# Attention scores in strips of 64 columns: another tiling of the products, another grouping of the heads, and the band's edge cleared by GpSimd for four units

## What is computed

```
dist = q_pos[:, :, None] - k_gpos[:, None, :]
allowed = (dist > 0) & (dist <= w) & (k_gpos[:, None, :] >= 0)
scores = jnp.einsum('bhnqd,bhnkd->bhnqk', qb, kb) * scale
scores = jnp.where(allowed, scores, NEG)
attn = jax.nn.softmax(scores, axis=-1)
out = jnp.einsum('bhnqk,bhnkd->bhnqd', attn, vb)
```

## Time and profile before

| | |
|---|---|
| median of 3 runs | 621.35 us (620.0 to 621.54) |
| the profiled execution: its time / its span | 620.31 us / 618.6 us |
| busy in the span: PE, DVE, POOL, ACT | 571.3, 448.0, 344.9, 290.6 us |
| mean granted TensorE clock | 0.965 of full |

### The profile page before, as it was taken

One profiled execution on the slowest core, in us unless ns is written; L12 is line 12 of the kernel. 1 busy time (PEld: TensorE's weight loads), 2 busy tenths in 40 slices (PEclk: granted clock), 3 DMA queues, 4 the chain that ended last, 5 costly groups with the idle time before them and its releaser, 6 DMA issues. The chain is left out here.

```text
span 618.6 us, 17277 instructions
## 1 busy us (share of the span) xinstructions
PE 571.3 (92%) x5504; PEld 390.2 (63%) x5509; DVE 448.0 (72%) x2031; ACT 290.6 (47%) x787; POOL 344.9 (56%) x749
## 2 busy tenths in 40 slices
PE   7898869979999999899999999987799999999992
PEld 3555336747777677577777777754367766776672
DVE  6884458838888888688888888885464767766646
ACT  1464305727676676567776767773132121212110
POOL 4664202637885878658888588898212242432251
PEclk9997979969999999899999999998999999999997
DMA  4586850633542454255433440000000000000001
GB/s 132 176 259 180 200 111 9 133 50 46 59 52 41 50 66 50 30 54 63 49 45 52 59 58 11 4 2 1 2 2 0 2 19 17 17 0 17 19 18 34
DMA packets 56590, 33.83 MB, mean 55 GB/s; under 512 B 5850, under 2 KB 55426, under 8 KB 56506
## 3 DMA queue, kind: packets, MB, share of 16 engines
q1 hardware_dynamic: 55450, 32.45, 29.0%
q10 hardware_dynamic: 1056, 0.35, 0.2%
HBM read 21.18 MB, written 11.27 MB: 52 GB/s over the span
## 5 line engine op out<-in xcount | busy, mean ns | idle before, releaser
L1036 DVE CUSTOM_DVE_ANT_0 added<-psS,maskq 128x256 bf16<-128x256 f32 x512 | 205.5, 412 | 61.1 <-PE psS L893 53.7
L1267 ACT ACTIVATE probs<-psST 128x512 f32<-128x512 f32 x256 | 154.0, 603 | 109.5 <-PE psST L914 108.3
L914 PE MATMUL psST<-qst,kst 98*128 98x128 bf16 x1024 | 101.7, 222 | 5.0 <-DMA qst<-mT 4.7
L914 PEld LDWEIGHTS psST<-qst,kst 98*128 98x128 bf16 x1024 | 79.1, 99 | 28.0 <-DMA qst<-mT 6.7
L893 PE MATMUL psS<-kst,qst 68*128 68x256 bf16 x448 | 88.6, 280 | 1.3 <-DVE rowmax L1036 0.8
L930 PE MATMUL psPV<-probs,vst 128*9 128x128 f32 x2048 | 82.2, 280 | 0.8 <-POOL probs L1182 0.4
L1179 POOL TENSOR_SCALAR_AFFINE_SELECT probs<-probs 128x256 f32<-128x256 f32 x140 | 57.9, 413 | 33.9 <-ACT probs L1267 33.7
L1700 ACT ACTIVATE hT<-fpsH 128x512 f32<-128x512 f32 x32 | 19.1, 598 | 121.6 <-PE fpsH L1444 121.6
L1182 POOL TENSOR_SCALAR_AFFINE_SELECT probs<-probs 128x256 f32<-128x256 f32 x140 | 57.4, 410 | 0.0
L893 PEld LDWEIGHTS psS<-kst,qst 68*128 68x128 bf16 x448 | 35.0, 102 | 33.7 <-issue 22.3
L1441 PE MATMUL fpsH<-xehi,w1hi 128*128 128x512 f32 x128 | 55.7, 435 | 0.0
(11 more groups left out here) (179 smaller groups left out, 1144.3 us busy)
## 6 DMA issues: line engine op xcount, KB each, us to landing
qst<-q_parts SPq DMA_DIRECT2D x96, 64.0 KB
kst<-k_parts SPq DMA_DIRECT2D x96, 64.0 KB
q_parts<-split SPq DMA_DIRECT2D x8, 384.0 KB, 2.7
k_parts<-split SPq DMA_DIRECT2D x8, 384.0 KB, 2.9
v_tok<-vt SPq DMA_DIRECT2D x8, 288.0 KB, 3.3
vst<-v_tok SPq DMA_DIRECT2D x16, 144.0 KB
X<-in_L_attn_x_dram SPq DMA_DIRECT2D x8, 256.0 KB, 3.0
out_dram<-res SPq DMA_DIRECT2D x8, 256.0 KB, 2.2
```

Source lines behind the costliest of these rows:

```text
L914: last = nc.tensor.matmul(bank[:, a, side * P:(side + 1) * P], kst[0:KALL, h, ring(n - 1 + side)], qst[0:KALL, h, ring(n)], start=not mask ...
L1036: taken = nc.vector.tensor_tensor_reduce(added[:, h], psS[g % 2][:, a], mask[:], 1.0, NEG * 4, ALU.add, ALU.max, rowmax[:, n.mod(2), h:h + 1])
L1267: nc.scalar.activation(probs[:, g], psST[g % 2][:].rearrange("p a c -> p (a c)"), ACT.Exp, scale=SCALE).then_inc(s_exp.sem, 1)
```

## The change

`scores` computes each head in two strips of 64 queries by 192 keys, the only keys that the band of such a strip can touch, instead of one 128 by 256. `scores_t` computes strips of 64 keys by 64 or 128 queries; the corners of a bank that no strip covers hold NEG, written once by DVE. The mask product covers the two 64-column edges only, and SELECTED has four units (0, 2, 4, 6). Units now pair other heads (`head_of`), so that `values` takes two heads at once: v of 18 columns by 256 probabilities, two calls of four units each (at g = 5 and at g = 1 of the next step) where there were four calls. The maximum reads 192 columns. Only the first block of each sequence is special, not every eighth. q, k and v are written to DRAM in another order and are loaded for four blocks at once in rows of 8 KB; for that the columns of the weights are rearranged by ten ACT copies, v's bias comes with eight DMAs, and `project` is no loop any more. The DMAs for the masks are small. Many waits and places move; those that the prediction speaks of are in the diff, cut to its core:

```diff
-LC = 2
+LC = 4
+SLOTS = RING // LC
+HALF = H // 2
 STORES = 16 * 4
-LOADS = 14
-PARTS_Q = [0, 0, 0, 1, 1, 2]
-PARTS_K = [0, 1, 2, 0, 1, 0]
+RUNS_Q = ((0, 0, 3), (3, 0, 2), (5, 0, 1))
+RUNS_K = ((0, 0, 1), (1, 0, 1), (2, 0, 2), (4, 1, 2))
+LOADS = 16 * (len(RUNS_Q) + len(RUNS_K))
...
+QD = 64
+QUADS = P // QD
+WIN = P + QD
 UN = H // 2
-SELECTED = (0, 2, 3, 4, 6)
+SELECTED = (0, 2, 4, 6)
 EPS = 1e-5
 LN_EPS = 1e-12
+
+
+def head_of(g, a):
+
+    return H // 2 * (g // 4) + 4 * a + g % 4
...
+def load_half(sp, c, half, side, held, scratch, s_half):
+
+    u, heads = c % SLOTS, slice(half * HALF, (half + 1) * HALF)
+    tile, runs = ((held.qst, RUNS_Q), (held.kst, RUNS_K))[side]
+    rows = scratch[side][c].rearrange("a (d h) t -> (a d) h t", h=H)[:, heads].rearrange("r h t -> r (h t)")
+    for first, part, parts in runs:
+        sp.dma_start(tile[first * HD:(first + parts) * HD, u, heads].rearrange("r h t -> r (h t)"),
+                     rows[part * HD:(part + parts) * HD]).then_inc(s_half[half][u], 16)
...
                 for a in range(2):
-                    h = 2 * g + a
-                    q = qst[0:KPROD, h, ring(n)]
-                    if n.mod(RING):
-                        last = nc.tensor.matmul(bank[:, a], q, kst[0:KPROD, h, ring(n - 1, 2)],
-                                                start=True, stop=True)
-                    else:
-                        nc.tensor.matmul(bank[:, a, 0:P], q, kst[0:KPROD, h, ring(n - 1)], start=True, stop=True)
-                        last = nc.tensor.matmul(bank[:, a, P:2 * P], q, kst[0:KPROD, h, ring(n)],
-                                                start=True, stop=True)
+                    h = head_of(g, a)
+                    for i in range(QUADS):
+                        q = part(qst, KPROD, n, h, QD * i, QD)
+                        if n.mod(LC):
+                            last = nc.tensor.matmul(bank[quad(i), a, 0:WIN], q, part(kst, KPROD, n - 1, h, QD * i, WIN),
+                                                    start=True, stop=True)
+                        else:
+                            nc.tensor.matmul(bank[quad(i), a, 0:P - QD * i], q,
+                                             part(kst, KPROD, n - (1 if n.k else 0), h, QD * i, P - QD * i),
+                                             start=True, stop=True)
+                            last = nc.tensor.matmul(bank[quad(i), a, P - QD * i:WIN], q,
+                                                    part(kst, KPROD, n, h, 0, QD * (i + 1)), start=True, stop=True)
...
-                masked = n.mod(RING) == 0 or g not in SELECTED
-                if masked:
-                    which = n.over(RING, 1, 1) if n.mod(RING) == 0 else 0
-                    nc.tensor.matmul(bank[:], identb[:],
-                                     maskk[:, which, :].unsqueeze(1).broadcast_to([P, 2, 2 * P]),
-                                     start=True, stop=False)
+                first = n.mod(BB) == 0
+                masked = first or g not in SELECTED
+                for j in range(QUADS) if masked else ():
+                    pick, sides = identb[:, quad(j)], slice(1, 2) if first else slice(0, 2)
+                    nc.tensor.matmul(bank[quad(j)].rearrange("p a (s q) -> p a s q", s=2)[:, :, sides, quad(j)], pick,
+                                     maskk[:, sides].unsqueeze(1).broadcast_to([P, 2, 1 if first else 2, QD]),
+                                     start=True, stop=False, skip_group_check=True)
                 for a in range(2):
-                    h = 2 * g + a
-                    for side in range(2):
-                        last = nc.tensor.matmul(bank[:, a, side * P:(side + 1) * P],
-                                                kst[0:KALL, h, ring(n - 1 + side)], qst[0:KALL, h, ring(n)],
-                                                start=not masked, stop=(not masked or (a == 1 and side == 1)))
+                    h = head_of(g, a)
+                    if not first:
+                        for j in range(QUADS):
+                            nc.tensor.matmul(bank[quad(j), a, 0:QD * (j + 1)], part(kst, KALL, n - 1, h, QD * j, QD),
+                                             part(qst, KALL, n, h, 0, QD * (j + 1)),
+                                             start=not masked, stop=True, skip_group_check=True)
+                    for j in range(QUADS):
+                        last = nc.tensor.matmul(bank[quad(j), a, P + QD * j:2 * P], part(kst, KALL, n, h, QD * j, QD),
+                                                part(qst, KALL, n, h, QD * j, P - QD * j),
+                                                start=not masked, stop=True, skip_group_check=True)
                 last.then_inc(s_ST.sem, 1)
...
-            def values(n, G):
-
-                pe.wait_ge(s_exp.sem, s_exp.after(n, 2 * G + 2))
-                cleared = [k + 1 for k, unit in enumerate(SELECTED) if unit // 2 == G]
-                if cleared:
-                    pe.wait_ge(s_sel.sem, s_sel.after(n, cleared[-1]))
-                if G == 0:
+            def values(n, half):
+
+                pe.wait_ge(s_exp.sem, s_exp.after(n, 4 * half + 4))
+                pe.wait_ge(s_sel.sem, s_sel.after(n, 2 * half + 2))
+                if half == 0:
                     pe.wait_ge(s_pvs.sem, s_pvs.after(n - 1))
-                for side in range(2):
+                sides = (0, 1) if n.mod(BB) else (1,)
+                for side in sides:
                     for t in range(4):
-                        unit, a = 2 * G + t // 2, t % 2
+                        unit = 4 * half + t
                         last = nc.tensor.matmul(
-                            psPV[32 * t:32 * t + VW, G * P:(G + 1) * P],
-                            vst[:, (n - 1 + side).mod(RING), 4 * G + t, :],
-                            probs[:, unit, (2 * a + side) * P:(2 * a + side + 1) * P],
-                            start=(side == 0), stop=(side == 1), skip_group_check=True)
+                            psPV[32 * t:32 * t + 2 * VW, 2 * half * P:2 * (half + 1) * P],
+                            vst[:, (n - 1 + side).mod(RING), 2 * unit:2 * unit + 2, :].rearrange("p a e -> p (a e)"),
+                            probs[:, unit].rearrange("p (a s q) -> p s a q", a=2, s=2)[:, side],
+                            start=(side == sides[0]), stop=(side == 1), skip_group_check=True)
                 last.then_inc(s_pv.sem, 1)
...
+                    if g == 1 and (s - 1).live:
+                        values(s - 1, 1)
+                    if g == 1 and (s + 1).live:
+                        n = s + 1
+                        pe.wait_ge(s_neg.sem, s_neg.after(n))
+                        pe.wait_ge(s_y.sem, s_y.after(s - 3))
...
+                    if g == 5 and s.live:
+                        values(s, 0)
...
+            for bank in psST:
+                nc.vector.memset(bank[:], NEG).then_inc(s_consts, 1)
...
-                h = 2 * g + a
-                taken = nc.vector.tensor_tensor_reduce(added[:, h], psS[g % 2][:, a], mask[:], 1.0, NEG * 4,
+                h = head_of(g, a)
+                taken = nc.vector.tensor_tensor_reduce(added[:, h], psS[g % 2][:, a, 0:WIN], mask, 1.0, NEG * 4,
...
-                    if (g, a) == (5, 0) and (s - 1).live:
+                    if (g, a) == (6, 1) and (s - 1).live:
                         n = s - 1
                         dve.wait_ge(s_den.sem, s_den.after(n))
                         nc.vector.tensor_tensor(both[:, n.mod(4), 0].rearrange("p (h e) -> p h e", h=H),
                                                 heads[:, :, 0:HD], rden[:].unsqueeze(2).broadcast_to([P, H, HD]),
                                                 ALU.mult).then_inc(s_local.sem, 1)
...
-                    if (g, a) == (6, 1) and (s - 1).live:
-                        n = s - 1
+                    if (g, a) == (0, 1) and (s - 2).live:
+                        n = s - 2
                         dve.wait_ge(s_gated.sem, s_gated.after(n))
                         nc.vector.tensor_reduce(z[:], gated[:], AX.X, ALU.add).then_inc(s_z.sem, 1)
...
                 if s.live:
-                    select(s, SELECTED[1])
-                    select(s, SELECTED[2])
-                    select(s, SELECTED[3])
+                    select(s, 0)
+                    select(s, 2)
+                if (s - 3).live:
+                    n = s - 3
+                    pool.wait_ge(s_yn.sem, s_yn.after(n))
+                    nc.gpsimd.tensor_tensor(X[:, n.times(1), :], X[:, n.times(1), :], yn[:],
+                                            ALU.add).then_inc(s_x1.sem, 1)
+                if s.live:
+                    select(s, 4)
                 if (s - 1).live:
                     n = s - 1
...
                                             both[:, n.mod(4)].rearrange("p a (h e) -> p a h e", h=H),
                                             glr[:].unsqueeze(2).broadcast_to([P, 2, H, HD]),
```

(9 more changed lines are left out.)

276 lines of the change are left out of this document (134 added, 142 removed).

## The result

The changed kernel takes 658.4 us, the median of 4 runs, where the kernel before takes 620.7 in the same rounds: a ratio of 1.062, interval 1.055 to 1.069, slower. Two further runs, not among the four, took 658.2 us and, at a mean clock of 0.898, 674.1. The forecast was 625 us in a range of 597 to 648. The profiled execution took 654.74 us, its span is 652.7, 34.1 us more than before.

The account below looks back on a forecast made before the run. The prediction took PE to bound the kernel before, and POOL's last select to hold `values` after, giving 10.55 us steps. Steps +4.9, head -0.7, turn 0 and start +0.5 summed to +4.7: 625 us, range 597 to 648.

Parts of the forecast that it names:

- Start: Before the first transposes: seven more weight DMAs and ten copies on ACT, taken as +0.5 us, between 0 and +4.
- The 31 steps: In `attend`: 25 ordinary steps at 10.55 us and six lighter ones, together 322.6 against 317.65, +4.9 us.
- lighter steps: First two, two at the second sequence's start, last two of the 31 steps: 9.8 us each, 58.8 in all.
- Rival 3: Slower: idle pieces in every step make some steps run at the lower clock, +20 us, 645; chance 0.06.
- What PE waits for: In a step, `values` waits 1.3 us for POOL's last select, starting 3.2 after unit 6's scores; step 10.55 us.
- Rival 1: Faster: PE's work binds, not the chain through POOL; 36 us off, 589; chance 0.26.
- small waits: PE's waits behind `values` in a step: 0.25 us at L1001 (mparts) and 0.4 us at psRem.
- PE's work: PE's busy time per step in `attend`: 8.65 to 8.9 us, where the same sum before gave 9.5; a unit 0.42.
- Rival 2: Slower: strips don't pay on PE, a unit costs 0.67 us, step 11.35, +20 to 22, 646; chance 0.12.
- Waits for mT's DMA: At `scores_t` in the steps: the waits, 11.4 us over 8 times before, counted as gone.
- Turn: From `project` to `attend`: loads double in bytes but go in 8 KB rows at 250 GB/s; 0, between -5 and +5.
- Head of `attend`: Stage before the steps: shorter maxima -1.7 us, two DVE memsets +1.0, together -0.7 us.

Follow-up runs that it names:

- `a_bvrow`: The changed kernel with v's bias loaded in one piece and ordered by two ACT copies; ratio 1.057 to the kernel before, against 1.062.
- `b_bqk`: The changed kernel with bq and bk loaded in the order of the kernel before, the eight broadcasts left; one run, 660.9 us.
- `f_turn`: The changed kernel with the second slot's loads issued by SP at the head of `attend`; one run, 657.0 us.
- `r_all`: The changed kernel with the opening of `n_open` and the select order of `c_sel5`; 629.0 us, median of 6, beside 612.8 of the kernel before.
- `g_wide`: The changed kernel with QD = 128, so without strips; step 10.68 us at full clock, the 31 steps 329.9 us.
- `q_wide5`: The changed kernel without strips (QD = 128) and with unit 5 cleared instead of unit 6; step 10.32 us, the 31 steps 324.3 us.
- `c_sel5`: The changed kernel with unit 5 cleared by GpSimd instead of unit 6; step 9.91 us, the 31 steps 317.2 us, span 638.4 us.
- `t_widel`: The changed kernel without strips, in the order of `l_order`; the 31 steps 324.9 us.
- `l_order`: The changed kernel with unit 5 cleared, four DVE maxima in a row, mparts ahead of `gated`, lexp later; step 9.70 us, 31 steps 321.4 us.
- `n_open`: The changed kernel with one-row v bias and the second slot's loads issued on ACT's queue; of 16.0 us at the first scores, 2.9 left at the end.

## Why the prediction was wrong, point by point

The profiled execution is 34.1 us over the one before, forecast 4.7. Of the 29.4 us between, the start has 11.8, the 31 steps 7.7, the turn 3.7, the stretch behind the last step 3.6 and the head of `attend` 3.0.

- **Start: the term that failed.** It was +0.5, between 0 and +4, reckoned by issue times alone, "PE waits for nothing before the first xn anyway". It measured 12.3. The wait is not for the issue, which ends 4.6 us later than before, but for the landing of the eight broadcasts, 2048 pieces of 32 bytes on a queue with brq behind them. `a_bvrow` and `b_bqk` show it. No row of before has such a DMA, and that the nearest, one broadcast of 512-byte rows, lands in time was no bound for it.
- **The 31 steps: the steady step right, the sum mis-sized.** 10.55 forecast, 10.45 measured; +4.9 forecast, +12.6 measured. The sum priced every ordinary step alike. It left out the seven long steps, 8.0 us over the steady one: the more work that DVE has between the maxima once in eight blocks, and in five of them a clock of 0.78 to 0.86. Of the lighter steps, put at 19.6 a pair, the first two took 18.7 and the last two 21.3; the pair at the start of the second sequence is among the long ones and took 22.5 (19.8 in `a_bvrow`, at a clock of 1.00). Rival 3 was the lower clock at 6 in 100; it came beside the forecast, not instead.
- **What PE waits for: the moment right, the engine half right.** `values` at 3.2 came out at 3.19, with the select 0.15 ahead. My chain went through DVE once, for local; it didn't follow the two banks of `scores`, where a maximum must end before the scores two units on can begin. Four maxima (units 6 and 7) with rden, local, lrs and y among them stand there, and end within 0.15 us of the select. Rival 1's price (36 us for a free POOL chain) was therefore wrong: freeing it brought 0.54 a step, 13 us in the 31 steps. The small waits were 0.21 at L1001 and 0.27 at psRem, forecast 0.25 and 0.4.
- **PE's work: right.** 8.65 to 8.9 forecast, 8.93 to 8.98 busy; a unit 0.37 (338.82 to 339.19) where I took 0.42; a call of `values`, 16 passes, 0.99 from its start to the next, for 1.1. PE's busy share in a steady step is 0.86 for 0.82. Rival 2 (strips don't pay: a unit 0.67) falls: the eight pairs of `scores_t` go in 0.18 (339.01 to 339.19). The estimate from the Trainium skill (TensorEngine Tiling (Array Packing), Restrictions, with TensorE: Matmul & The Clock Gate, LDWEIGHTS), 0.43 us for eight loads in a row, does not hold here. But what PE's work is worth was not tested by the forecast: the strips alone are 0.23 to 0.52 us per step at full clock, and 0 to 7 us in the 31 steps of one execution, less than the runs of one kernel differ.
- **Waits for mT's DMA: right**, none is left in the steps.
- **Turn: within its bounds**, +3.7 in -5 to +5. As a whole it moved 205 GB/s at a share of 0.80, near the rate assumed. But the second slot's loads alone, in `f_turn`, moved 94 to 105 GB/s at a share of 0.92 to 1.05, not 250, and in the changed kernel the last stores stand behind them on SP's queue: with them out of the way the first scores come 6.5 us earlier.
- **Head of `attend`: -0.7 forecast, +2.3**, with the clock at 0.77 there against 0.87. **Behind the last step: 0 forecast, +3.6**: the longest waits of PE are 3.04 us for `mixed` and 1.49 at `values`, where rows of before have 1.80. The cause of either was not tested.

## What to carry to other kernels

A one-time load is not free because it is small: read what waits for the last of the weights, and how many DMAs and pieces stand ahead of it, before the bytes. Where two chains through different engines end within 0.2 us at one instruction, shortening one moves that instruction by no more than 0.2 (here 0.02), and what else it brings lies behind it (here 0.4 at L1001); list for each wait all its releasers, the reuse of banks too. A microsecond won ahead of a wait must be followed to the end of the program: of 16 us at the opening, one kernel kept 3 and another 12.

## What the runs showed of the hardware

- The same kernel ran at a mean clock of 0.937 to 0.965, and its time moved with it from 631.6 to 614.7 us (`r_all`), more than most edits here bring.
- In all three orders the kernel without strips ran at the higher mean clock (over the whole program, all runs): `g_wide` 0.945 to 0.959, the changed kernel 0.898 to 0.942; `q_wide5` 0.941 to 0.965, `c_sel5` 0.920 to 0.941; `t_widel` 0.937 to 0.957, `l_order` 0.910 to 0.920. PE's busy share does not tell it: in a step at full clock it is 0.91 in `g_wide` (steps at 1.00) and in `l_order` (steps at 0.93), and PE busy over 0.93 stayed at 0.50 for 25 us in `n_open`. Why the clock does not rise there, and rises after 8 us in the changed kernel, stays open.
- A DMA share near 1 is not a rate: the loads of the second slot, mostly q and k into 8 to 24 partitions, moved 94 to 105 GB/s at 0.92 to 1.05 (`f_turn`), stores and loads mixed in `project` 197 at 0.70 (the changed kernel).
